# Gated unit's first product and two norms' rows on GpSimd, query bias and prototype exponentials on ScalarE, in a fused PixArt block with routed experts

## The reference, cut to what matters

```python
# layer 0, on x of (4, 1024, 256)
h = ln(x) * (1 + sc_msa) + sh_msa
x = x + g_msa * window_attention(h)        # 16 heads of 16, windows of 128 shifted by 64
h = ln(x) * (1 + sc_mca) + sh_mca
x = x + g_mca * topk_cross_attention(h, ctx)   # 77 keys, the best 16 kept per row and head
h = ln(x) * (1 + sc_mlp) + sh_mlp
u = h @ w_m1 + b_m1                        # 256 -> 2048, halves a and b
x = x + g_mlp * ((silu(a) * b) @ w_m2 + b_m2)
# layer 1
nx = layer_norm(x)
weights = softmax(nx @ Wq @ (ctx @ Wk).T / 16)      # over 77 prototypes
evidence = weights @ (ctx @ Wv)
combined = concat(nx, evidence, cond)
routed = sum over 3 experts of softmax(combined @ router_W) * (silu(combined @ e_w1) @ e_w2)
g = sigmoid(silu(combined @ gate_w1) @ gate_w2)
return x + g * (routed @ out_w + out_b)
```

## Time and profile before

| | |
|---|---|
| median of 3 runs (1461.56 to 1464.62) | 1461.87 us |
| the profiled execution | 1469.42 us |
| its span | 1467.6 us |
| TensorE clock granted, mean, of full speed | 0.99 |

### The profile page before, as it was taken

How to read it: one execution, slowest core, us unless ns; L and a number is a source line. 1 busy time by engine, 2 the same in 40 slices (tenths; PEclk the granted TensorE clock), 3 DMA queues, 4 the chain that set the end, 5 groups by cost and what they waited for, 6 DMA issues and landing times.

```text
span 1467.6 us, 31028 instructions
## 1 busy us (share of the span) xinstructions
PE 1406.1 (96%) x10145; PEld 1176.2 (80%) x10145; DVE 1074.2 (73%) x4909; ACT 816.7 (56%) x2523; POOL 437.0 (30%) x599
## 2 busy tenths in 40 slices
PE   7989999999999999999999999999999999998997
PEld 5778788887888788787888778888887878887886
DVE  3485869688786878878696777869688786968632
ACT  2473374746557374655747466574747547474433
POOL 1314132323325232331334232232334313232302
PEclk9999999999999999999999999999999999999999
DMA  7520000010000000010010000000010000000000
GB/s 240 179 86 2 1 1 25 2 34 9 19 30 15 2 2 25 2 34 1 19 37 1 16 1 16 11 16 19 8 47 2 15 2 2 8 1 8 1 1 15
DMA packets 27346, 35.06 MB, mean 24 GB/s; under 512 B 3324, under 2 KB 22448, under 8 KB 26929
## 3 DMA queue, kind: packets, MB, share of 16 engines
q1 hardware_dynamic: 27185, 33.07, 7.3%
HBM read 28.83 MB, written 4.22 MB: 23 GB/s over the span
## 4 chain that ended last, share of the span: by engine, by line
PE 64%; DVE 28%; issue 5%; ACT 1%; SPq 1%; DMA 1%; DVEq 0%; POOL 0%; ACTq 0%; POOLq 0%
PE bank L1034 10%; PE bank L1010 10%; DVE knocked L2288 8%; PE bank L965 8%; PE bank L1017 6%; PE bank L804 6%; PE bank L853 3%; DVE M L2276 3%; DVE M L2281 3%; PE bank L974 3%; PE bank L843 2%; PE bank L790 2%; DVE gT L2308 2%; PE bank L865 2%; PE bank L761 2%
## 5 line engine op out<-in xcount | busy, mean ns | idle before, releaser
L965 PE MATMUL bank<-hB,Wm 128*128 128x256 f32 x1024 | 244.3, 385 | 2.2 <-ACT hB L1413 2.2
L965 PEld LDWEIGHTS bank<-hB,Wm 128*128 128x128 f32 x1024 | 191.5, 191 | 34.1 <-issue 7.5
L1010 PE MATMUL bank<-nxT,W1nx 128*128 128x256 f32 x896 | 214.0, 385 | 3.4 <-ACT probT L1467 3.0
L1452 ACT ACTIVATE prob<-bank,rmax 128x128 f32<-128x128 f32 x512 | 179.5, 404 | 29.8 <-DVE rmax L2210 29.8
L1811 POOL TENSOR_TENSOR scores<-scores,M 128x308 f32<-128x308 f32 x128 | 94.4, 737 | 334.6 <-DVE knocked L2288 332.3
L1010 PEld LDWEIGHTS bank<-nxT,W1nx 128*128 128x128 f32 x896 | 166.7, 191 | 28.9 <-ACT probT L1467 5.5
L1034 PE MATMUL bank<-W2p,gT 128*128 128x256 f32 x768 | 183.2, 381 | 3.0 <-DVE acc L2372 1.9
L1034 PEld LDWEIGHTS bank<-W2p,gT 128*128 128x128 f32 x768 | 141.2, 190 | 23.8 <-issue 2.8
L1505 ACT ACTIVATE tbs<-bank,b1half 128x256 f32<-128x256 f32 x128 | 60.7, 474 | 146.4 <-PE bank L965 98.2
L1521 ACT ACTIVATE tbs<-bank,betaH 128x256 f32<-128x256 f32 x224 | 96.6, 498 | 78.4 <-PE bank L1017 78.4
L1803 POOL TENSOR_SCALAR vare<-mv 128x2 f32<-128x2 f32 x64 | 17.6, 275 | 389.9 <-DVE mv L2186 387.4
(11 more groups left out here) (256 smaller groups left out, 2823.8 us busy)
## 6 DMA issues: line engine op xcount, KB each, us to landing
Wm_g<-in_L_xcond_w_m_dram SPq DMA_DIRECT2D x4, 1024.0 KB, 5.5
W1ev<-in_L_xcond_e_w_dram SPq DMA_DIRECT2D x6, 512.0 KB, 7.6
x<-in_x_dram SPq DMA_DIRECT2D x16, 128.0 KB, 2.4
x<-in_x_dram SPq DMA_DIRECT2D x32, 64.0 KB, 2.4
Wm<-in_L_xcond_w_m_dram SPq DMA_DIRECT2D x1, 2048.0 KB, 8.7
out_dram<-acc SPq DMA_DIRECT2D x16, 128.0 KB, 1.7
out_dram<-acc SPq DMA_DIRECT2D x32, 64.0 KB, 2.1
batch_rows<-row_store SPq DMA_DIRECT2D x4, 384.0 KB, 3.9
```

Of the source, the lines that this page charges most:

```text
L965: m = pe.matmul(bank_of(name)[:, half * UT:(half + 1) * UT], Wm1[:, k, c:c + P], hB[:, k, :], start=(k == 0), stop=(k == CB - 1))
L1010: pe.matmul(bank_of(name)[:, n * UT:(n + 1) * UT], W1nx[:, k, c0 + n * P:c0 + (n + 1) * P], nxT[:, k, :], start=(n == 0 and k == 0), stop= ...
L1452: m = act.activation(prob[:, s, i, :], psum[s][:, i * P:(i + 1) * P], ACT.Exp, bias=rmax[:, t, s * HPS + i:s * HPS + i + 1], accum_out=rsu ...
```

## The change

GpSimd makes (tanh + 1) * a in two instructions, tanh * a into `tb` and the sum with a into `gT`; this is taken out of DVE's `b_swiglu`, except in `last_experts`, where DVE still makes it. ACT's wait for a free `tb` follows this product instead of the drained bank. GpSimd also applies norms 0 and 3 in `both` (in `last_cross` and `last_experts` norm 3 stays on DVE). ACT writes the biased and scaled query from its bank, and takes the prototype exponentials from their bank with the negative maximum as bias and their sums as by-product; the scale 1/16 goes into `GpR`. The orders on all engines are rewritten around this, and `r2` moves from bank 1 to bank 3.

```diff
-    ["c01", "c11", "v", "y01", "y11", "r2", "rt", "s01", "p01", "s11", "p11", "g2"],
+    ["c01", "c11", "v", "y01", "y11", "rt", "s01", "p01", "s11", "p11", "g2"],
-    ["c03", "c13", "y00", "y10", "s03", "p03", "s13", "p13", "hg"],
+    ["c03", "c13", "y00", "y10", "r2", "s03", "p03", "s13", "p13", "hg"],
...
 # PE, both
                 b_first_evidence("h00", 0, b)
-                b_first_nx("h11", RH + 2 * P, b)
                 b_first_evidence("h01", 2 * P, b)
                 a_turn_picked(1, 0, c)
                 a_turn_picked(1, 1, c)
-                b_first_evidence("h10", RH, b)
                 a_turn_picked(1, 2, c)
                 a_turn_picked(1, 3, c)
+                b_first_evidence("h10", RH, b)
+                a_turn_inverses("r2", "xv", c)
+                b_router(b)
+                a_cross_values(1, c)
+                b_first_nx("h11", RH + 2 * P, b)
+                a_scores(0, range(SLOTS), a)
                 b_first_evidence("h11", RH + 2 * P, b)
-                a_turn_inverses("r2", "xv", c)
-                a_cross_values(1, c)
-                b_router(b)
-                a_scores(0, range(SLOTS), a)
...
 # ACT
+            def a_scale_queries(u):
+                wait_full(act, "q", u)
+                for f in range(CB):
+                    i = act.activation(qT[:, f, :], bank_of("q")[:, f * UT:(f + 1) * UT], ACT.Identity,
+                                       bias=qbias[:, f:f + 1], scale=float(D) ** -0.5)
...
                 elif j >= 2:
-                    wait_drained(act, f"m{j - 2}", u)
+                    act.wait_ge(half_gated, u * HJ + (j - 1))
...
             def b_proto_exp(u):
-                wait_drained(act, "ps", u)
-                act.activation(pw[:, :, :], pw[:, :, :], ACT.Exp, scale=float(C) ** -0.5).then_inc(proto_exp, 1)
+                wait_full(act, "ps", u)
+                act.wait_ge(proto_max, u + 1)
+                act.wait_ge(route_nx, u + 1)
+                for t in range(TILES):
+                    i = act.activation(pw[:, t, :], bank_of("ps")[:, t * (LC + E):t * (LC + E) + LC], ACT.Exp,
+                                       bias=pm[:, t:t + 1], accum_out=psu[:, t:t + 1])
+                i.then_inc(drained[JOB["ps"][0]], 1)
...
 # ACT, both
                 a_cross_exp(0, 1, c)
+                a_kept_exp(0, c)
                 a_keys(a)
+                a_scale_queries(a)
                 a_copy_values(a)
...
 # POOL
+            def ln_apply(i, src, dst, u):
+                pool.wait_ge(rstds[i], u * 2 + 2)
+                for t in range(TILES):
+                    pool.tensor_scalar(dst[:, t, :], src[:, t, :], mv[i][:, t, 0:1], rstd[i][:, t:t + 1], ALU.subtract, ALU.mult)\
+                        .then_inc(normed[i], 1)
+            def b_half_swiglu(j, u):
+                name = f"m{j}"
+                t = tb[tb_of(name)][:, 0:UT]
+                pool.wait_ge(tanh_done, u * len(TANH_ORDER) + (TANH_ORDER.index(name) + 1))
+                pool.tensor_tensor(t, t, gated_of(u)[:, j, :], ALU.mult).then_inc(tanh_weighted, 1)
+                pool.wait_ge(tanh_weighted, u * HJ + (j + 1))
+                pool.tensor_tensor(gated_of(u)[:, j, :], gated_of(u)[:, j, :], t, ALU.add).then_inc(half_gated, 1)
...
 # POOL, both
                 add_bias(1, xc, c)
+                b_half_swiglu(0, b)
                 a_shift(0, 0, c)
+                b_half_swiglu(1, b)
+                rstd_of(0, EPS0, a)
                 a_shift(0, 1, c)
-                rstd_of(0, EPS0, a)
+                b_half_swiglu(2, b)
+                a_shift(0, 2, c)
+                b_half_swiglu(3, b)
+                wait_full(pool, "ln2", a - 1)
+                ln_apply(0, xa, xnA, a)
+                a_shift(0, 3, c)
+                b_half_swiglu(4, b)
+                b_half_swiglu(5, b)
+                b_half_swiglu(6, b)
+                b_half_swiglu(7, b)
                 if r == 3:
                     gate_so(batch)
                 if r == 0:
                     gate_co(batch)
-                a_shift(0, 2, c)
-                a_shift(0, 3, c)
                 add_bias(0, xa, a)
-                rstd_of(3, EPS1, b)
                 a_shift_kept(0, c)
                 a_shift(1, 0, c)
+                rstd_of(3, EPS1, b)
+                ln_apply(3, xb, xnB, b)
...
 # DVE
             def b_swiglu(j, u):
                 name = f"m{j}"
-                w = tb_of(name)
-                dve.wait_ge(tanh_done, u * len(TANH_ORDER) + (TANH_ORDER.index(name) + 1))
-                dve.scalar_tensor_tensor(gated_of(u)[:, j, :], tb[w][:, 0:UT], 1.0, gated_of(u)[:, j, :], ALU.add, ALU.mult).then_inc(half_gated, 1)
                 dve.wait_ge(half_gated, u * HJ + (j + 1))
...
 # DVE, both
                 b_swiglu(3, b)
-                wait_full(dve, "ln2", a - 1)
-                ln_apply(0, xa, xnA, a)
                 b_swiglu(4, b)
...
                 b_swiglu(6, b)
+                a_topk("b", 0, 3, c)
                 b_swiglu(7, b)
...
                 ln_stats(3, xb, b)
-                a_topk("b", 0, 3, c)
-                ln_apply(3, xb, xnB, b)
                 a_pick(0, 1, c)
                 a_topk("a", 1, 1, c)
-                a_bias_queries(a)
                 a_topk("b", 1, 0, c)
                 a_topk("a", 1, 2, c)
+                a_topk("b", 1, 1, c)
+                a_topk("a", 1, 3, c)
                 b_proto_shift(b)
-                a_topk("b", 1, 1, c)
+                a_topk("b", 1, 2, c)
                 b_proto_norm(b)
-                a_topk("a", 1, 3, c)
-                a_topk("b", 1, 2, c)
                 a_topk("b", 1, 3, c)
...
                 b_silu("h00", hE[:, 0], 0, b)
+                b_route_shift(b)
                 a_normalise("xv", oT2, c)
-                b_route_shift(b)
```

More of the change, by code:

```diff
@@ L189, in bass_pixart_experts @@
         kbias = sb("kbias", [P, PAR, CB])
+        qbias = sb("qbias", [P, CB])
         neghalf = sb("neghalf", [P, TILES])
@@ L1439, in a_keys @@
                 i.then_inc(drained[JOB["k"][0]], 1)
+            def a_scale_queries(u):
[3 more added lines that the diff above has]
+                                       bias=qbias[:, f:f + 1], scale=float(D) ** -0.5)
+                    if f == 0:
+                        i.then_inc(q_half, 1)
+                i.then_inc(drained[JOB["q"][0]], 1)
             def a_copy_values(u):
@@ L1670, in both @@
                 a_copy_picked(0, 2, c)
+                a_cross_exp(1, 0, c)
                 b_proto_exp(b)
-                a_cross_exp(1, 0, c)
+                a_cross_exp(1, 1, c)
                 b_copy_weights(b)
-                a_cross_exp(1, 1, c)
-                a_kept_exp(0, c)
+                a_kept_exp(1, c)
                 if r == 1:
@@ L2070, in helpers @@
                 chain(dve.tensor_scalar(b1half[:, :], cols[:, COLS["m1"]:COLS["m1"] + HJ], 0.5, None, ALU.mult))
+                chain(dve.tensor_scalar(qbias[:, :], cols[:, COLS["qkv"]:COLS["qkv"] + CB], float(D) ** -0.5, None, ALU.mult))
                 for e, m in enumerate((maskE, maskO)):
@@ L2301, in a_pick, with b_half_swiglu @@
                 dve.scalar_tensor_tensor(main, K[:, g, 0:MAIN], KNOCKED_BELOW, Dx[:, t, g, 0:MAIN], ALU.is_lt, ALU.mult).then_inc(picked, 1)
+            def b_half_swiglu(j, u):
+                name = f"m{j}"
+                dve.wait_ge(tanh_done, u * len(TANH_ORDER) + (TANH_ORDER.index(name) + 1))
+                dve.scalar_tensor_tensor(gated_of(u)[:, j, :], tb[tb_of(name)][:, 0:UT], 1.0, gated_of(u)[:, j, :], ALU.add, ALU.mult).then_inc(half_gated, 1)
             def b_swiglu(j, u):
                 name = f"m{j}"
-                w = tb_of(name)
-                dve.wait_ge(tanh_done, u * len(TANH_ORDER) + (TANH_ORDER.index(name) + 1))
-                dve.scalar_tensor_tensor(gated_of(u)[:, j, :], tb[w][:, 0:UT], 1.0, gated_of(u)[:, j, :], ALU.add, ALU.mult).then_inc(half_gated, 1)
                 dve.wait_ge(half_gated, u * HJ + (j + 1))
@@ L2322, in b_proto_shift @@
                 v = both[:, :, 0:LC]
-                dve.tensor_reduce(pm[:, :], v, AX.X, ALU.max).then_inc(proto_max, 1)
+                dve.tensor_reduce(pm[:, :], v, AX.X, ALU.max, negate=True).then_inc(proto_max, 1)
                 dve.tensor_tensor(rn[:, :, :], both[:, :, LC:LC + E], rbias[:, :].rearrange("p (a e) -> p a e", a=1).to_broadcast([P, TILES, E]), ALU.add)\
                    .then_inc(route_nx, 1)
-                dve.wait_ge(proto_max, u + 1)
-                dve.tensor_tensor(pw[:, :, :], v, pm[:, :].rearrange("p (t a) -> p t a", a=1).to_broadcast([P, TILES, LC]),
-                                  ALU.subtract).then_inc(drained[JOB["ps"][0]], 1)
             def b_proto_norm(u):
-                dve.wait_ge(proto_exp, u + 1)
-                dve.tensor_reduce(psu[:, :], pw[:, :, :], AX.X, ALU.add).then_inc(proto_steps, 1)
-                dve.wait_ge(proto_steps, u * 3 + 1)
+                wait_drained(dve, "ps", u)
```

(2 more changed lines are left out.)

18 lines of the change are left out of this document (9 added, 9 removed).

## The result

The changed kernel takes 1561.99 us (median of 4 runs, 1557.67 to 1564.43), the kernel before 1462.01 beside it. The ratio is 1.0669, 95% interval 1.0636 to 1.0702. The forecast was 1492, in a range of 1442 to 1520: slower, as predicted, but by 100 us and not by 30, outside the range.

The account below looks back on a forecast made before the run. TensorE, 96% busy, was taken as the bound. A new bank wait of 3.1 us less old waits gave 1.29 a pass, 18 us, plus 12 for the clock: 1461.9 + 30 = 1492 us, range 1442 to 1520.

Parts of the forecast that it names:

- The chain from the first tanh pair to the fifth `b_swiglu`: Loop pass: GpSimd's products in series with choice, shifts and norm 0, 16.80 us together, ending 3.6 us late.
- the factor of 1.6 of the rows: GpSimd's add at 0.73 us against VectorE's product spaced by 0.45, used instead of the skill's factor of about two.
- The first rival: At the bank hand-over of the first norm, GpSimd's products keep up: faster, 1437 us; chance 0.24.
- the price of a norm: Norms on GpSimd, between copy and add: 0.57 us a tile, 1.14 a norm, ends 0.80 and 1.46.
- 3.1: TensorE's new wait per pass, in us, at the turn of `xnA`, for bank 0 to be freed by the fifth `b_swiglu`.
- its rows may come late to TensorE: Norm 3 on GpSimd: late by up to 1.14 us, taken as 0 because TensorE comes 3.1 later.
- a wait at `xnB`: Sign of being wrong: TensorE waiting elsewhere than at the turn of `xnA`, as at that of `xnB`; no size given.
- the fall in seven passes of fourteen: Clock drop behind TensorE's new wait at `xnA`: 7 x 1.7 = 12 us, ends 0 and 26.
- The third rival: Dearer: clock falls in every pass, 1506 us, or GpSimd's steps near 913 ns, 1531 with both; chance 0.19.
- The waits for `pw`, `rl` and `kept`: TensorE's old loop waits, expected to go: 0.54, 0.83 and 0.44 us a pass, 25 us in 14 passes.
- the prototype exponentials on ScalarE at nothing: Two exponentials start behind the maximum, covered by a VectorE group of 1.39 us; without cover, 0.33 a pass more.
- The wait of `last_cross`: Long wait of 3.55 us there, expected shorter by the group moved away; taken as 0 between -3 and +3.

Follow-up runs that it names:

- norm3_back: The changed kernel with norm 3 alone back on VectorE, behind its first pick of tile 0; products and norm 0 stay on GpSimd: 1559.42 us, ratio 1.0648.
- filled: The changed kernel with TensorE making the seventh hidden block three times, two thrown away, in front of the turn of `xnA`: 1541.51 us, ratio 1.0510.
- all_back: The changed kernel with products, both norms and the old order of the choice back on VectorE; ScalarE's query and exponentials and TensorE's order stay: 1465.05 us, ratio 1.0002.
- norm3_only: The changed kernel with products and norm 3 back on VectorE, norm 0 on GpSimd, the choice in the changed order: 1469.67 us, ratio 1.0012.
- norms_back2: The changed kernel with norms 0 and 3 back on VectorE, norm 3's inverse deviation placed as in the changed kernel; products stay on GpSimd: 1498.54 us, ratio 1.0202.

## Why the prediction was right and wrong

**Right: the path.** The chain from the first tanh pair to the fifth `b_swiglu` was forecast at 16.80 and took 18.30 (587.91 + 0.47 to 606.20 + 0.48); 1.29 of the difference is norm 0. Its two ends in the changed kernel:

```profile
587.91 0.47 ACT L1519 ACTIVATE gT<-bank,cols 128x256 f32<-128x256 f32 x1
```

```profile
606.20 0.48 DVE L2369 SCALAR_TENSOR_TENSOR gT<-bank,cols,gT 128x256 f32<-128x256 f32 x1 [4.09 <-POOL gT L1867]
```

Bank 0 decides at the turn of `xnA`, not the rows. A step on GpSimd took 0.73, its longest 0.74, so the factor of 1.6 of the rows held. The factor of about two in the Trainium skill, "GPSIMD Engine Reference", section "Engine selection", was not reached by the products. The first rival, that they keep up, is false. The prediction had read the Trainium skill, "Perfetto Trace Analysis", section "Optimizing Scalar/DVE Operations", too strongly for it: the section says that such a move may make sense and, for the shared port, that it might not help.

**Wrong, first: the price of a norm.** The step reads "so I take the middle, 0.57 a tile, 1.14 a norm, with the ends 0.80 and 1.46". It measured 1.22 a tile, 2.43 a norm, above the upper end, which was an add of two tensors. No row of before showed an operation with columns on GpSimd at this size, and I took the copy and the add for bounds; they are not. With 2.43 the wait comes to 3.1 + 1.3 = 4.4 in the pass that I laid out, where it was 4.48. Over 14 passes it was 53.2, and 3.1 x 14 is 43: 10 us of the miss. The Trainium skill, in the same section of "GPSIMD Engine Reference", puts GpSimd's operations with one input at roughly line rate; the trace disagrees, 1.22 where VectorE took 412 ns in the median of its `xnA` tiles before.

**Wrong, second: norm 3.** The step reads "its rows may come late to TensorE by up to their own 1.14; I take 0, since TensorE comes 3.1 later". It measured 27.8 us. TensorE's lateness is no cover, because VectorE is late too: its statistics end 12.0 after the turn of `xnA` (606.74 to 618.76; before, 8.8). Of these 3.2 us, 2.1 are there at the last gated block already (6.4 behind the turn, before 4.3). Its hidden block comes behind the turn, in this pass at the lower clock, GpSimd's product follows in series, and VectorE stands 1.44 for it. The other 1.1 are VectorE's picks behind it, slowed as the last section shows. GpSimd's 4.3 follow in series. `norm3_back` shows that GpSimd's price is not the whole of it: with norm 3 on VectorE the rows still come late. The prediction named a wait at `xnB` among its signs of being wrong.

**Wrong, third: the clock.** "I take the fall in seven passes of fourteen". Slow products followed 13 of the 14 turns; the first of them (eight of 128x256 or four of 128x512, 1.9 us at full speed) took 2.8 to 3.6. In five passes the clock fell once more behind the turn of `xnB` (0.50 from 349 to 351, from 714 to 716, from 806 to 808, from 994 to 996 and from 1086 to 1088), which the prediction didn't have. TensorE's busy time grew by 31.6 us where I had 12 and an upper end of 26; `filled`, which touches the turn of `xnA` alone, gives back 20 to 23. The third rival had the fall in every pass and a chance of 0.19.

**Right in name only: the relief.** The waits for `pw`, `rl` and `kept` went, 25 us as counted, though the 6.2 for `kept` were the weight loads' and not all TensorE's. `all_back` shows that they can't be banked: without GpSimd's part the same change is level, because other waits of a few tenths take their place.

**Left out: bank 4.** I costed the prototype exponentials on ScalarE at nothing, named their cover, and didn't name who waits for them: the drain of `ps` moves from VectorE's subtraction to ScalarE, with `xv` behind it. In the changed kernel TensorE is too late to notice; in `norm3_only` it is 12.3 us. The wait of `last_cross`, which was to get shorter than 3.55, got longer, 5.0 (within the 3 allowed for it).

So 30 forecast and 88 in the spans: 10 from the longer bank wait, 28 from norm 3, 20 from the clock make up the difference. This says where TensorE lost the time, not what each part gives back: norm 3 alone gives back 3 us (`norm3_back`), since another wait takes its place. That the kernel without the norms on GpSimd loses 30 us (`norms_back2`) is luck and no confirmation of the sum, which had the norm in it.

## What to carry to other kernels

Before work is moved to an engine with room, write down whose queue it enters and which bank or buffer the instruction behind it frees: here the engine was 43% busy and still in the way, since every product stood in series with the choice. Place a moved instruction where that engine stands idle, by the timeline; one norm moved by two jobs was worth 45 us. A price that no row shows isn't bounded by operations of other forms, and where TensorE must stand, even thrown-away products can be cheaper than the clock that it loses.

## What the runs showed of the hardware

- On GpSimd an operation with one tensor and two columns (1.22 us for 128x256) is dearer than an add of two tensors (0.73), and with one column still 0.93.
- The length of TensorE's wait alone doesn't tell whether the clock is lower behind it: behind two waits of 2.12 us in one run it was once and once not, and in the changed kernel a wait of 3.28 was followed by eight products in 1.89.
- VectorE's picks, two tensors from SBUF each, slow down beside GpSimd's adds: in the changed kernel 28 of the 77 picks that overlap a GpSimd instruction are over 1.2 times their median, and none of the 115 others. Before and after, the same instruction (minimum, median, maximum in ns), and one pick of each kind on VectorE's timeline:

```profile
L2301 DVE SCALAR_TENSOR_TENSOR picked_first<-knocked,scores x32: 676/680/687, 81.7 to 1356.3; 128x512 f32<-128x512 f32 x32
```

```profile
L2356 DVE SCALAR_TENSOR_TENSOR picked_first<-knocked,scores x32: 679/685/1228, 76.9 to 1440.2; 128x512 f32<-128x512 f32 x32
```

```profile
614.48 1.11 DVE L2356 SCALAR_TENSOR_TENSOR picked_first<-knocked,scores 128x512 f32<-128x512 f32 x1
...
618.93 0.69 DVE L2356 SCALAR_TENSOR_TENSOR picked_first<-knocked,scores 128x512 f32<-128x512 f32 x1
```

The first lies beside GpSimd's bias adds and kept shift. The Trainium skill, "SBUF — State Buffer", section "SBUF: two separate sides", says that an operation of VectorE with two inputs from SBUF and one of GpSimd that reads SBUF exclude each other for a whole instruction. The trace agrees in kind; by the means of the two groups (812 and 319 ns, before 681 and 214, in 32 and 64 instructions) it is 10.9 us of VectorE in the whole run, ahead of the residual that norm 3 waits for.
